# Second norm of the feed-forward block: G times gamma plus beta summed in PSUM by TensorE products, and read there by ScalarE and VectorE

## The reference

```python
def act_quant(x):      # 127 levels per row, by the row's largest absolute value
    scale = 127.0 / clip(max(abs(x), axis=-1), 1e-5)
    return clip(round(x * scale), -128, 127) / scale
def bitlinear158(x, w, b):
    return einsum('bsd,od->bso', act_quant(rms_norm(x)), weight_quant(w)) + b
h = silu(bitlinear158(x, w1, b1))        # 256 -> 1024
h = gelu(h)
h = layer_norm(h, ln_g, ln_b)            # (h - mean) * rstd * ln_g + ln_b, over 1024
x = layernorm(x + bitlinear158(h, w2, b2))
```

## Time and profile before

| | |
|---|---|
| median of 3 executions | 534.74 us (532.0 to 537.67) |
| profiled execution, its own time | 532.01 us |
| its span, first to last instruction | 530.2 us |
| mean granted clock of PE in the span | 0.878 |
| busy in the span: PE, DVE, ACT, POOL | 80%, 83%, 70%, 55% |

### The profile page before, as it was taken

How to read it: one execution, slowest core, us unless ns; L and a number is a source line. 1 busy time by engine, 2 the same in 40 slices (tenths; PEclk the granted TensorE clock), 3 DMA queues, 4 the chain that set the end, 5 groups by cost and what they waited for, 6 DMA issues and landing times. The chain is left out here.

```text
span 530.2 us, 11850 instructions
## 1 busy us (share of the span) xinstructions
PE 425.0 (80%) x4098; PEld 230.1 (43%) x4098; DVE 439.5 (83%) x942; ACT 370.4 (70%) x690; POOL 294.2 (55%) x407
## 2 busy tenths in 40 slices
PE   6558799999999999999999999988996602555554
PEld 5344455455555454545555545443432201333332
DVE  3855687989889898798999999888877869999993
ACT  2231257678687786777868778677769878999983
POOL 5741646475474754647447475487242147667653
PEclk9886699999999999999999999999999855555557
DMA  7132223252442523324243232222000000000001
GB/s 230 42 83 56 79 69 91 52 152 62 135 122 64 151 71 86 115 58 143 65 129 117 63 113 64 79 71 62 3 2 1 1 0 0 14 29 20 30 32 40
DMA packets 52460, 37.05 MB, mean 70 GB/s; under 512 B 21553, under 2 KB 47793, under 8 KB 52401
## 3 DMA queue, kind: packets, MB, share of 16 engines
q1 hardware_dynamic: 52112, 36.06, 23.4%
q10 hardware_dynamic: 288, 0.23, 0.1%
HBM read 24.48 MB, written 10.49 MB: 66 GB/s over the span
## 5 line engine op out<-in xcount | busy, mean ns | idle before, releaser
L871 ACT ACTIVATE PB<-e_b 128x512 f32<-128x512 f32 x256 | 148.2, 592 | 59.1 <-PE e_b L683 58.0
L1065 DVE TENSOR_REDUCE MX<-mx_b 128x2 f32<-128x512 f32 x256 | 166.7, 678 | 26.8 <-PE mx_b L655 25.6
L655 PE MATMUL mx_b<-KA,QA 48*128 48x256 bf16 x512 | 98.1, 278 | 11.2 <-DVE MX L1065 10.5
L683 PE MATMUL e_b<-QA,KA 50*128 50x256 bf16 x512 | 97.2, 274 | 0.4 <-ACT PB L871 0.2
L700 PE MATMUL u_b<-PB,VA 128*32 128x256 f32 x1024 | 84.0, 391 | 2.1 <-ACT PB L871 1.7
L992 POOL TENSOR_TENSOR SP<-SP,srec 128x1024 f32<-128x1024 f32 x15 | 28.5, 1901 | 77.8 <-DVE srec L1037 77.8
L655 PEld LDWEIGHTS mx_b<-KA,QA 48*128 48x128 bf16 x512 | 29.8, 94 | 86.7 <-issue 47.1
L1405 PE MATMUL r_b<-identh,Q 128*128 128x128 f16 x128 | 16.2, 305 | 39.5 <-ACT Q L1318 39.5
L1411 PE MATMUL z_b<-w2q,Q2T 128*128 128x256 bf16 x128 | 28.5, 400 | 19.3 <-ACT Q2T L1329 19.3
L982 POOL TENSOR_TENSOR KM<-QK,att_tab 128x512 f32<-128x512 f32 x31 | 32.0, 1052 | 21.2 <-ACT QK L825 21.2
L560 PE MATMUL g_b<-XT,wp 128*128 128x128 f32 x256 | 34.4, 290 | 4.6 <-DMA wp<-in_wpT 4.6
(11 more groups left out here) (188 smaller groups left out, 1018.3 us busy)
## 6 DMA issues: line engine op xcount, KB each, us to landing
KA<-parts_k SPq DMA_DIRECT2D x64, 96.0 KB
QA<-parts_q SPq DMA_DIRECT2D x64, 96.0 KB
parts_q<-part_q SPq DMA_DIRECT2D x32, 128.0 KB, 1.9
parts_k<-part_k SPq DMA_DIRECT2D x16, 192.0 KB, 2.1
C<-in_ctx SPq DMA_DIRECT2D x16, 128.0 KB, 3.5
X<-in_x SPq DMA_DIRECT2D x16, 128.0 KB, 2.9
out_y<-O SPq DMA_DIRECT2D x16, 128.0 KB, 1.7
XT<-in_xT SPq DMA_DIRECT2D x15, 128.0 KB, 2.2
```

The costliest lines, as they stand in the source:

```text
L655: m = nc.tensor.matmul(mx_b[n % 2][:, D * k:D * k + D], QA[low:low + K_MAX, 2 * i.ring + b, h, P * u:P * u + P], KA[low:low + K_MAX, 2 * i ...
L683: m = nc.tensor.matmul(e_b[n % 2][:, D * k:D * k + D], KA[low:low + K_EXP, 2 * i.ring + b, h, P * sc:P * sc + P], QA[low:low + K_EXP, 2 * ...
L871: nc.scalar.activation(PB[:, n % 4].rearrange("p e t -> p (e t)"), e_b[n % 2][:, :], ACT.Exp, scale=XC ** -0.5).then_inc(e_sb.sem, 1)
L1065: nc.vector.tensor_reduce(MX[:, b, e, 2 * q:2 * q + 2, u], mx_b[n % 2][:, :].rearrange("p (e s) -> p e s", e=2), AXL.X, ALU.max).then_inc( ...
```

## The change

In the second block, h times gamma plus beta no longer ends in SBUF. POOL still multiplies by gamma in SBUF; the sum with beta is made by PE in a PSUM tile `n_b` of two banks (three such tiles, in a ring): a bf16 product of `sel` and `BP` writes beta into all 128 rows, and an f32 product of the identity and h is added on it (`row_sum`). DVE's largest value, ACT's sum of squares and ACT's rounding read `n_b`. DVE's plus-beta is gone. Shift and scale is done by ACT for even pairs only, and for odd pairs by one DVE instruction (`scale_h`). The lags shrink, 24 turns in place of 25. `r_b` and `z_b` have one bank each in place of two. `BP` holds beta as three bf16 parts in partitions 0, 32 and 64; POOL makes them in the first block, in the iterations 10, 11 and 12 of its loop over pairs (`row_parts`). Two roundings on ACT use `Copy` with a constant in place of `Identity` with a bias from a tile.

```diff
@@ POOL, first block
+            def row_parts(steps):
+                mid, low, own = slice(32, 64), slice(64, 96), slice(0, 96)
...
+                    if k == 0:
+                        ins = nc.gpsimd.memset(sel[:], 0.0)
+                    elif k < 4:
+                        ins = nc.gpsimd.memset(sel[32 * (k - 1):32 * (k - 1) + 1], 1.0)
+                    elif k == 4:
+                        pool.wait_ge(ld_rows, 16 * 4)
+                        ins = nc.gpsimd.tensor_copy(BP[own], bet[own])
+                    elif k == 5:
+                        ins = nc.gpsimd.tensor_tensor(BR[own], bet[own], BP[own], ALU.subtract)
...
+                if i.v in (10, 11, 12):
+                    wait(pool, split["q"], j, 5)
+                    row_parts((range(0, 5), range(5, 8), range(8, 10))[i.v - 10])
@@ second block
-        LAG_G, LAG_N, LAG_Z = 1, 5, 7
+        LAG_G, LAG_N, LAG_Z = 1, 4, 6
@@ ACT, second_values(t)
+                if i := pair_at(t, 4):
+                    wait(act, ymax, i, 1)
...
+                    nc.scalar.activation(SQ[:], n_b[i.ring][:, :], ACT.Square, accum_out=sc[:, i.v, 0:1]).then_inc(sqr.sem, 1)
...
-                    nc.scalar.activation(Q2[:, j.p, :], row_h(j), ACT.Identity, bias=rnd16[:],
+                    nc.scalar.activation(Q2[:, j.p, :], n_b[j.ring][:, :], ACT.Copy, bias=ROUND16,
                                          scale=sc[:, j.v, 6:7]).then_inc(qd.sem, 1)
...
+                if (i := pair_at(t, 2)) and i.p == 0:
+                    act.wait_ge(shift.sem, i.v // 2 + 1)
+                    nc.scalar.activation(row_h(i), row_h(i), ACT.Identity, bias=nmh[:, i.v // 2 % 2, 0:1],
+                                         scale=root[:, (i.v + LAG_G) % 4, 0:1]).then_inc(s_even, 1)
@@ POOL, turn(t)
-                if i := pair_at(t, 4):
-                    wait(pool, yn, i, 1)
-                if (i := pair_at(t, 3)) and i.v != NPAIR - 1:
-                    wait(pool, zs, i, 1)
-                    nc.gpsimd.tensor_tensor(row_h(i), row_h(i), gam, ALU.mult).then_inc(zg.sem, 1)
+                i = pair_at(t, 2)
+                if i and i.p == 1 and i.v != NPAIR - 1:
+                    product(i)
...
+                if i and i.p == 0:
+                    product(i)
@@ PE
+            def row_sum(i):
+                if has(i, 3):
+                    wait(pe, qd, i.plus(-3), 1)
+                for c in range(2):
+                    nc.tensor.matmul(n_b[i.ring][:, 512 * c:512 * c + 512], sel[:], BP[:, 512 * c:512 * c + 512],
+                                     start=True, stop=False)
...
+                    wait(pe, zg, i, 1)
+                for c in range(2):
+                    m = nc.tensor.matmul(n_b[i.ring][:, 512 * c:512 * c + 512], ident, row_h(i)[:, 512 * c:512 * c + 512],
+                                         start=False, stop=True)
...
+            for t in range(TURNS2):
+                if (i := pair_at(t, 3)) and i.p == 0:
+                    row_sum(i)
+                if j := pair_at(t, 5):
+                    numbers(j)
+                if (i := pair_at(t, 2)) and i.p == 1:
+                    row_sum(i)
+                if j:
+                    second_product(j)
@@ DVE
-                nc.vector.tensor_tensor(row_h(j), row_h(j), bet, ALU.add).then_inc(yn.sem, 1)
+            def scale_h(g, prev):
+                nc.vector.tensor_scalar(row_h(g), row_h(g), mvh[:, g.p, 0:1], prev[:, 0:1],
+                                        ALU.subtract, ALU.mult).then_inc(s_odd, 1)
+                if g.v == NPAIR - 1:
+                    dve.wait_ge(s_odd, NPAIR // 2)
+                    nc.vector.tensor_tensor(row_h(g), row_h(g), gam, ALU.mult).then_inc(s_last, 1)
...
+                if g and g.p == 1:
+                    scale_h(g, prev)
```

More of the change, by code:

```diff
@@ L1276, in build_layer @@
         es = outer
-        r_b = [bank(f"r_b{n}", F16) for n in range(2)]
-        z_b = [bank(f"z_b{n}") for n in range(2)]
+        tail_banks.close()
+        n_b = [es.enter_context(nc.psum_tensor(f"n_b{n}", [P, INNER], F32)) for n in range(3)]
+        r_b, z_b = bank("r_b", F16), bank("z_b")
         block = es.enter_context(nc.Block())
         last = Pair(0, NPAIR - 1)
-        TURNS2 = NPAIR + 9
+        TURNS2 = NPAIR + 8
         def row_h(i):
@@ L1305, in second_values @@
             def second_values(t):
[L1306 to L1313, removed]
+                if i := pair_at(t, 4):
+                    wait(act, ymax, i, 1)
+                    if has(i, 1):
+                        wait(act, sqr, i.plus(-1), 1)
+                    nc.scalar.activation(SQ[:], n_b[i.ring][:, :], ACT.Square, accum_out=sc[:, i.v, 0:1]).then_inc(sqr.sem, 1)
+                j = pair_at(t, 5)
                 if j:
@@ L1398, in first_product, with numbers @@
                 m.then_inc(f_ps.sem, 1)
+            def row_sum(i):
[4 more added lines that the diff above has]
+                                     start=True, stop=False)
+                if i.v == NPAIR - 1:
+                    pe.wait_ge(s_last, 1)
+                else:
+                    wait(pe, zg, i, 1)
+                for c in range(2):
+                    m = nc.tensor.matmul(n_b[i.ring][:, 512 * c:512 * c + 512], ident, row_h(i)[:, 512 * c:512 * c + 512],
+                                         start=False, stop=True)
+                m.then_inc(n_ps.sem, 1)
+            def numbers(j):
+                wait(pe, qd, j, 1)
+                if has(j, 1):
+                    wait(pe, q2_sb, j.plus(-1), 1)
+                for k in range(8):
+                    m = nc.tensor.transpose(r_b[:, P * k:P * k + P], low_half(Q2[:, j.p, P * k:P * k + P]), identh[:])
+                m.then_inc(q2_ps.sem, 1)
             def second_product(j):
-                wait(pe, qd, j, 1)
-                if has(j, 2):
-                    wait(pe, q2_sb, j.plus(-2), 1)
+                wait(pe, q2_sb, j, 1)
+                if has(j, 1):
+                    wait(pe, zn, j.plus(-1), 1)
                 for k in range(8):
[L1405 to L1410, removed]
-                    m = nc.tensor.matmul(z_b[j.p][:, 0:D], Q2T[:, j.p, k, :], w2q[:, k, :], start=k == 0, stop=k == 7)
+                    m = nc.tensor.matmul(z_b[:, 0:D], Q2T[:, j.p, k, :], w2q[:, k, :], start=k == 0, stop=k == 7)
                 m.then_inc(z_ps.sem, 1)
@@ L1487, in z_sum @@
                     wait(dve, on, z.plus(-3), 1)
-                nc.vector.scalar_tensor_tensor(out=Z[:, z.ring, :], in0=z_b[z.p][:, 0:D], scalar=sc[:, z.v, 7:8],
+                nc.vector.scalar_tensor_tensor(out=Z[:, z.ring, :], in0=z_b[:, 0:D], scalar=sc[:, z.v, 7:8],
                                                in1=XALL[:, z.v, :], op0=ALU.mult, op1=ALU.add).then_inc(zn.sem, 1)
@@ L1510, in turn @@
                     row_ceiling(f, prev)
-                if g:
+                if g and g.p == 0:
                     shift_h(g, prev)
```

73 lines of the change are left out of this document (42 added, 31 removed).

## The result

Median of the kernel before 533.49 us (532.0 to 537.67, 4 runs), of the changed kernel 538.02 us (537.25 to 539.45, 4 runs): ratio 1.0088, 95% interval 1.005 to 1.0127. The change costs about 4.7 us. The profiled execution of it took 537.25 us, its span is 535.5 us, against 532.01 and 530.2. All ratios here leave out three slow executions (552.75 us in x2, 637.22 in x7, 582.87 of the kernel before), while the medians given for x2 and x7 count theirs.

What follows compares the result with a forecast made beforehand. DVE was taken to set the pace, ACT just behind. Terms of +4.7, +0.4, -4.3, +2 for the clock and -0.3 for ACT gave +2.5 us: 534.5 profiled, median 537, forecast's own range 534 to 541, whole range 528 to 545.

Steps and rivals of the forecast that it cites:

- The hold: In odd turns DVE's scaling waits some 1.4 us for POOL's even product to end, then takes 0.70 us.
- The chain: In the last stage, dependent steps alternating between DVE and POOL make two turns 11.0 us, against 10.9 before.
- Turns 2 to 8: Start of the last stage, where turns were short: 29.2 us for 24.45, +4.7.
- Turns 8 to 16: Middle of the last stage: four times 11.0 us for 43.64, +0.4.
- Turn 16 to pair 13: Late in the last stage, up to pair 13's factors, now in turn 18: 11.1 us for 15.38, -4.3.
- The clock: TensorE's row sums at half clock: +1 for the first, +1 for one or two later ones.
- What follows 512.79 the change hardly alters: Behind pair 13's factors, a chain of steps per pair was taken as nearly unchanged.
- `row_parts`: POOL's beta parts in the attention stage: 4.8 us in a gap of 5.46 us, taken as 0.
- 9.8 if these two decided: Two turns of the last stage would take 9.8 us if DVE and ACT alone set the pace.
- The first: Rival: TensorE at half clock in most pairs of turns, each costing 1 to 1.7 us; 541 to 546, chance 0.27.
- The second: Rival: the odd scaling is not held by POOL; 10.3 us for two turns, 532, chance 0.18.
- third: Rival: DVE and ACT set the pace after all; two turns at 9.8 us, 526 to 529, chance 0.12.

Runs made afterwards that it cites:

- x2: The changed kernel with DVE scaling odd pairs after its statistics, sum with x and bases, and POOL making root before the odd product; 544.34 us, ratio 1.0181.
- x7: The changed kernel with extra unread TensorE products only at the start, 24 ahead of the first row sum and 32 ahead of the third; 536.68 us, ratio 1.0052.
- x1: The changed kernel with the odd pair's scaling written as a scalar_tensor_tensor whose second operand is the root column repeated; 539.74 us, ratio 1.0103.
- x4: The changed kernel with odd pairs without POOL's product: DVE multiplies by gamma, TensorE multiplies with a root-scaled diagonal; 538.86 us, ratio 1.0099.
- x5: The changed kernel with one row sum each turn, their readers a turn later, root before POOL's products and DVE's odd scaling last; 522.03 us, ratio 0.9805.
- x9: x5 with one thing put back, DVE's scaling of the odd pair early in its turn; 536.23 us, ratio 1.0071.
- x3: The changed kernel with extra unread TensorE products at the start, in even turns and in the drain; 532.63 us, ratio 0.9984.
- b1: The kernel before with 12 extra unread TensorE products in each turn ahead of its w2 product; 531.7 us, ratio 0.9974.
- x8: x5 with DVE's odd scaling early again and POOL's odd product ahead of O and root, as in the changed kernel; 537.36 us, ratio 1.0081.

## Why the prediction held, and where its sum did not

- **The bound and the forecast** (+2.5 us, 537): the direction and the mechanism held; measured +5.3 us in span, +4.7 as ratio, 538.02. The loss is about twice the forecast, and what is missing is the clock (below).
- **The hold** ("the scaling lasts about 2.1 us, ending with POOL's product"): 2.07 us, and x1 and x4 show by the fixed time behind POOL's end that it is a hold, x5 and x9 that it costs what it lasts. What the scaling needs by itself is 0.81 us and not 0.70. The 2.1 came out of two small misses that cancel: from its start to the end of POOL's product it is 1.51 us and not 1.4, and from there to its own end 0.55 and not 0.70.
- **The chain** (11.0 us for two turns, alternating 4.4 and 6.6): 10.93, 4.34 and 6.59. But the prediction laid the time to the chain through POOL, with the odd product in it. x4 and x9 correct this: without the odd product ahead of root a pair still takes 10.64 us. DVE's own lost 1.26 us nearly suffice (9.38 + 1.26), and the odd product ahead of root adds 0.29.
- **Turns 2 to 8, +4.7**: measured +7.05. The structure was right (29.2 expected, 28.9 in x3, where every row sum runs at full clock); the other 2.6 us are half clock, for which I charged +1 here.
- **Turns 8 to 16, +0.4**: +1.21, of which 1.1 is clock. **Turn 16 to pair 13, -4.3**: -4.02.
- **The clock, +2 in all**: this is the term that was mis-sized. It cost 6.2 us by x3, of which the kernel before paid 0.8 as well (b1). I had priced only row sums in the turns. The rows behind it have a small misreading: the unbroken work ahead of the rise at 520.1 is 2.7 us (517.01 to 519.75), not 2.9. "What follows 512.79 the change hardly alters" is the step that failed outright: that part became 1.42 us longer (17.41 to 18.83), and there the clock fell in the drain (the w2 products at 524.55 and 528.41 take 1.89 us), where before it had risen at 520.1. Extra products bring this part to 16.75 us in x3 and 16.4 in b1, so the step would have held at full clock.
- **`row_parts`, 0**: right, 1.13 us of its gap were left.
- **DVE 9.1 and ACT 9.6 to 9.8, "9.8 if these two decided"**: x5 runs at 9.38 with DVE at 48.81 of 50 us and ACT at 46.01, which is 8.6 us a pair; ACT's need was put too high.
- **Rivals.** The first (half clock in most pairs, 541 to 546) came half true. Five of the eight odd turns had a row sum at half clock, which is where I let it begin, but in the middle such a pair took 11.34 to 11.65 us, 0.4 to 0.7 more than 10.93, and not 1 to 1.7. (By its own terms, +0.8 and seven times 1 to 1.7, that rival came to 542.5 to 547.4, not 541 to 546.) The second (no hold) and third (faster) are excluded for this kernel; x5 shows the third's end, reached by orders and not by the change as it stands. What the change took from DVE, 1.14 us a turn, was real: it was given back as the hold, as root behind a product, and as clock.

What stays open: why a profile's first shift lies at 428 to 430 us or at 431 to 432, which moves single spans by up to 3.7 us; what share the hold has when the odd product still stands ahead of root; and whether transposes hold the clock up, which no run here separates from the w2 products.

## What to carry to other kernels

When work moves from one engine to another, look up what the other engine of the pair VectorE and GpSimd does at that moment: do not let wide SBUF instructions of the two meet. A VectorE scaling with a single wide operand was held just as one with two; what ran unhindered beside GpSimd's products here were its statistics, and beside GpSimd's root its largest value read from PSUM. Also put small results that others wait for (here root) ahead of wide products in the queue. Work laid on a TensorE at half clock is paid at half clock where it lies, and so is what follows it; give its readers a turn to spare before paying for extra products. A cure that moves one wait (x2) is judged only when the next wait has been removed as well: the same two orders were 1.8% slower without a turn's slack and 2% faster with it.

## What was not expected of the hardware

- A scalar_tensor_tensor whose second operand is one column repeated is held by POOL's product like one with a full row: 2.61 and 2.60 us, both ending 1.1 us behind the product.
- A three-column power on POOL was held by a 0.80 us scaling on DVE: 1.34 in place of 0.85 us.
- VectorE's largest value over 1024 columns takes 1.22 us from PSUM and 1.21 from SBUF, and ScalarE's square 1.02 and 1.04.
- The same list on TensorE, a row sum each turn, ran at clock 1.00 in x5 (pair of turns 9.38 us, TensorE busy 40.12 of 50 us), at 0.97 in x9 (10.64 us) and at 0.88 in x8 (10.93 us), each from 450 to 500. The changed kernel, with two row sums every second turn, had 0.92 there.
